# A decoder kernel whose five engines follow written-out orders: the orders, and the hand-out of PSUM banks, written anew

## The chip, the cores and the metric

The kernel runs on one core of a Trainium2 chip. The metric is the time of one launch in device microseconds (us). The kernel before took 5946.84 us, the median of three runs (5941.74 to 5958.27).

## What is computed

The reference is a four-layer decoder over 64 sequences of 128 tokens with 128 channels, all in float32. Each of twelve stages is added to its input and normalised over the channels:

```python
x = _layernorm(x + stage(x, ...), axis=-1)      # twelve times, one stage after the other
```

The stages are, in order and by the names that the kernel uses:

- `rec`: a recurrence over the tokens, solved beforehand for all sequences in an opening phase; of it only a few products are left for the main phase.
- `x0`, `x1`, `x2`: attention with 16 heads of 8 channels from the 128 tokens to a context of 77 rows. `a2`, `a3`, and the first half of `f3`: the same from the tokens to themselves (128 keys).
- `a1`: latent attention with 8 heads, causal. `x3`: attention without a softmax.
- `f0`: a mixture of 8 experts, each taking its 32 best tokens. `f1`: a feed-forward stage with inputs rounded to 4-bit levels. `f2`: a low-rank stage with 6 experts.
- `f3`, second half (`ex`): 8 experts on all tokens, 128 to 512 to 128 channels each.

## The kernel before

**Groups and batches.** After an opening phase (the first 470 us, not touched by the change) the 64 sequences are worked as 16 batches of 4. Three groups of buffers exist, called 0, 1 and 2. Batch i belongs to group i mod 3, so group 0 works six batches one after the other, and groups 1 and 2 five each. Within a group one batch is a single long chain: every stage needs the normalised output of the one before. Work of different groups is independent, and what hides the waits inside one group's chain is the work of the other two.

**Steps.** For each engine a generator (`whole_tensor`, `whole_scalar`, `whole_vector`, `whole_gpsimd`, `whole_sync`) issues one group's instructions in steps, each ended by a `yield`. A batch has 329 steps on TensorE, 255 on ScalarE, 556 on VectorE and 27 on GpSimd. A step begins with its waits on semaphores and then issues one or several instructions.

**The order.** An engine executes its instructions in the order in which they are issued, so one string per engine fixes how the groups' steps stand between one another. `in_order` reads it letter by letter and takes the next step of the group that the letter names:

```python
    for who in order:
        next(programs[who], None)
```

The strings are in the dictionary `ORDER` (line 250). TensorE's has 5264 letters (329 x 16), VectorE's 8896, ScalarE's 4080, GpSimd's 432. SyncE's has 624; there the letters `a` and `b` stand for the two streams of expert weights (256 KB a piece, four places each, `stream_sync`, line 2927), for `f0` and for `ex`. Nothing at run time chooses: if the first instruction of a step must wait, everything behind it on its engine waits as well, of whichever group.

**Banks.** The eight PSUM banks are given out in four pairs. `rec`, `f0`, `a1`, `f1`, `x3` and `ex` take one pair for a group, the other seven stages two. The string `GIVEN` (line 454) lists in pairs of digits which group takes which pair next; `take_banks` (line 1298) makes TensorE wait for the last read by the previous owner.

**Attention.** `attention_tensor` (line 1511) goes through the four sequences of a batch. For each: `scores` (line 1527, 8 matmuls by rows of 32), four maxima on VectorE (`top`, line 1620), the transposition of the maxima (`tops turned`, line 1540), their subtraction from the queries on VectorE (`q shifted`, line 1623), the scores again in the other orientation (`shifted`, line 1555), four exponentials on ScalarE (`p`, line 1607), the product with the values (`out`, line 1577), a copy on ScalarE (`oT`, line 1601), transpositions (`by tokens`, line 1588), and a reciprocal and a product on VectorE (lines 1637 and 1640).

**Experts.** In `gated_tensor` (line 2633) a `hidden` step is one product with 512 columns (line 2646), taken up by ScalarE (line 2674) or VectorE (line 2686) in turn; after each of them stands a quarter of an `expert` step, four products with 128 columns (line 2661). `f0` has similar steps at lines 1902 and 1912. These two kinds of stage are called expert stages below.

Of the kernel before, what the change touches and what calls it, by code (L numbers as in the profile page):

```python
# [212 lines left out]
def memory_layouts(w):  # L213
# [38 lines left out]
        "0000000000000000000000000000000000000000000000000000000000101011111000100101001010101100110010111001"  # L252
        "1001011001110010110000000101001000010100011101122010001101121121121100110111221212220010011001100102"
        "1111210211200112121012002001102212112221121212011200120120110201101000101101000101110010200120110100"
        "1210110020200022012000112011220110002202210100022022221222020002210102000010011200110122122211220000"
        "0100100201221221111212211112211012201011201000122011000220202000101010202102101200122010101101212121"
        "1122112021012020202100202220202022002011110100100110100010110201120120220222200111011011011012021020"
        "1010000210022121021020001000111001000010011010001001100201000202100010211200020210001201002120200200"
        "1002012202112112121222211112122121212111221211211212122001201020102220200202102102021011010101110110"
        "0011011101110010110110110210110210121221112112112201112102121102112111012110110110100110012102122012"  # L260
        "1012000022200200020000202112010020010210201210020222100211002202020221001021002122120010101201202110"
        "2010001110101010120101210220022020202020002021012021222211211121011021122112110020020020211211110111"
        "2121002221211201211002012122002202121010221102202221120102211022022020211212202221201220002221120122"
        "2001022122122221122112212221200102202100121101011011001010111010120021022220200002210202110121201102"
        "1122222221221222120002020121101120120010001100212011121212110220010020100221200112212222222201221021"
        "2022110201001011202202202220022020020201022121022010122012102211122102102012011212120220210100120012"
        "1022002200202202200200220220202002010110101001121122122012210212101000002000000100110020021001101120"
        "0202211220020000202000002002020002000020022200200002002220020022100212210020021221211221112121221121"
        "1222121001210222102111220020120120101020220220200202202002200221010001102101010100111012102120222122"
        "1121210010101100100121001010212000010100012000122012101212211211211011210200202010121121210211121121"  # L270
        "2102011021210210111211010101110210112121200212210211100112211100110211220201121102200200202022202020"
        "0202211201001110102210112002202020202102221221222122121221022201012121022102202001220221121212210212"
        "1221221202202221212220210202200220220122220111011110011011011111102120211200122102110202020202021001"
        "1200112201210120021122121122221121202112002211010011021120120001011201200101122022220012022021012222"
        "2222112121222101000110101011100101012012202202022221210112010211010100022020002200220201022000001220"
        "1000202021020110110122102012100010121122111212122111212212210101200202201012121012120010101001101010"
        "0011101000100101201120210221122122101020101011201210101010021010212010020102120020000202000002001221"
        "1021001021102022100210100200020020200020020010200201002201022000021221212121221211122122112112122100"
        "1201210200110222210100101020222020200222002002202210201001110111001010012122121222102021121101001100"
        "1001001210010120120000100100201202012101021212211211112102211201101211200210212101101211211200101110"  # L280
        "0112112120012101111010112112100112022110220112111112020111012220200202221120112002220200221120210201"
        "0110202000222020020202202202202212222222221222222202122202222022022022022002222221221222222221022221"
        "1011110101121221201220010210210201202020200022202000202220200020222010201002201000120122010111101011"
        "0120112111121011000111201212020200222011100110120122102222112222010020121022002002110100110022022122"
        "1221112221012001200001001010122200221011000220200022002200020200120210102002121201100101121122111122"
        "1221010120020200202020222020202012110100011011100000200202201012212202010110010101012000010100201002"
        "0010010010020100200021110200010022001001001010001001002100100210200010200202110010102121221221121212"
        "2212111201202210112102122100120100120120202022000202220200002202200020220210211201100111212221211212"
        "1210202202220102101010110010100112002100221000212000210020202101212121112122121112122121021010100201"
        "1020221210022012020122200022010212110101012201220221100210110121112211221212111212201021001200120220"  # L290
        "0220020210212020010110121012000110211011201101111111111111111010100110101001101111111101111111101012"
        "1121101100201211201202202222020202200220222012202102102220122110210212210021022020221222120120202102"
        "1022012122021211212212212212112101101011000012210200210220202102020101101112011012012110111111212112"
        "1121020022020202022002202121002112112101001112211121120200202001001020222022211202202222102222210012"
        "0201101001110122202221001012020012202100100221010220120121211221020212001010110221211202122002022002"
        "0220002022202220200020020202210202121121111100000100022002212001220022000010011001002110010020021001"
        "0000120122012021200100011010010001001100100100100120100021121000201211212112212211212122211121220012"
        "0101001220211102101022102002020002202020002202200020200200220221211121001212101110101100100202202200"
        "0000212121001010102010001102102121122012100101000011101001001210212012012201012210102101120020001212"
# [3084 lines left out]
```

## Time and profile before

| | |
|---|---|
| median of three runs | 5946.84 us |
| the profiled execution's own time | 5938.98 us |
| its span, first to last instruction | 5937.1 us |
| TensorE busy with matmuls | 5049.5 us, 85% |
| VectorE busy | 3616.8 us, 61% |
| ScalarE busy | 2391.6 us, 40% |
| mean granted clock of TensorE | 0.913 |

The span is one execution. An engine is busy while it works on an instruction; TensorE's matmuls overlap one another and the loading of weights, so its busy time is not its time at full speed. The granted clock is the share of 2.4 GHz that TensorE was given: it is either 1.0 or 0.5 at a moment, and a mean over a stretch lies between.

### The profile page before, as it was taken

To read this page: it belongs to the slowest core of one execution; us is meant where nothing else is said; L and a number is where in the kernel's file an instruction comes from. 1 tells how busy PE (TensorE), PEld (TensorE's weight loads), DVE (VectorE), ACT (ScalarE), POOL (GpSimd) and SP (SyncE) were. 2 spreads that over 40 slices of the span, in tenths; PEclk is the share of its full clock that TensorE was granted. 3 is DMA by queue.
4 is the path that set the end of the run, shared out by engine and by line. 5 is a ranking of instruction groups with operands and counts; after the bars stand their busy time and mean duration, and the time that the engine had idled before them with its cause. 6 is when DMAs were issued, how large, how long until landed. Compare 5 with 4: busy or idle time off the path is not lost.

```text
span 5937.1 us, 132505 instructions
## 1 busy us (share of the span) xinstructions
PE 5049.5 (85%) x56241; PEld 3711.9 (63%) x56241; DVE 3616.8 (61%) x9657; ACT 2391.6 (40%) x4612; POOL 715.0 (12%) x735
## 2 busy tenths in 40 slices
PE   4756788899898898998789898889889988988897
PEld 3544666567676666766666666756666765665664
DVE  7562567655666666566665665666666566656553
ACT  2112344443434444344344533443543444443431
POOL 6351001101001001000001100000100100000000
PEclk7666799999998999999899999999999988998997
DMA  1112000012010000111001111101001210100010
GB/s 56 25 46 91 30 12 19 7 33 66 13 45 11 30 28 12 56 38 43 26 2 38 32 36 38 58 2 31 19 19 35 64 34 3 36 23 1 14 47 25
DMA packets 144939, 184.71 MB, mean 31 GB/s; under 512 B 46074, under 2 KB 73826, under 8 KB 143714
## 3 DMA queue, kind: packets, MB, share of 16 engines
q1 hardware_dynamic: 144354, 176.23, 9.9%
q8 instruction: 450, 7.37, 0.5%
q14 instruction: 135, 1.11, 0.1%
HBM read 164.32 MB, written 11.57 MB: 30 GB/s over the span
## 4 chain that ended last, share of the span: by engine, by line
PE 67%; DVE 14%; ACT 6%; issue 3%; DMA 1%; POOL 1%; SPq 0%; DVEq 0%; POOLq 0%; ACTq 0%
PE g_bank L2646 8%; PE g_bank L2661 7%; PE g_bank L1555 6%; PE g_bank L1577 6%; PE g_bank L1527 5%; DVE g_tops L1620 4%; ACT g_keys_exps L1607 3%; PE g_bank L1588 3%; PE g_bank L1497 2%; PE g_bank L1902 2%; PE g_bank L2385 2%; PE g_bank L1436 2%; PE g_bank L1993 2%; PE g_bank L1912 1%; PE g_bank L2247 1%
## 5 line engine op out<-in xcount | busy, mean ns | idle before, releaser
L1620 DVE TENSOR_REDUCE g_tops<-g_bank 128x4 f32<-128x308 f32 (+1 forms) x1536 | 812.5, 575 | 413.6 <-PE g_bank L1527 410.9
L1607 ACT ACTIVATE g_keys_exps<-g_bank 77x512 f32<-77x512 f32 (+1 forms) x1536 | 800.3, 596 | 610.8 <-PE g_bank L1555 610.3
L1370 POOL TENSOR_TENSOR g_rstd<-g_rstd,minus_half 128x4 f32<-128x4 f32 x224 | 230.8, 1031 | 4288.9 <-DVE g_rstd L1352 4288.5
L2661 PEld LDWEIGHTS g_bank<-region,g_keys_exps 128*128 128x128 f32 x4096 | 520.4, 192 | 187.8 <-issue 178.9
L2646 PE MATMUL g_bank<-g_xT,region 128*128 128x512 f32 x1024 | 554.7, 624 | 21.8 <-DVE g_keys_exps L2686 12.0
L2661 PE MATMUL g_bank<-region,g_keys_exps 128*128 128x128 f32 x4096 | 545.4, 278 | 11.0 <-DVE g_base L2693 10.7
L1555 PE MATMUL g_bank<-g_qa,g_keys_exps 32*77 32x128 f32 (+1 forms) x12288 | 479.7, 296 | 84.3 <-DVE g_o L1640 55.6
L1555 PEld LDWEIGHTS g_bank<-g_qa,g_keys_exps 32*77 32x77 f32 (+1 forms) x12288 | 400.7, 178 | 197.7 <-DVE g_o L1640 79.0
L1577 PE MATMUL g_bank<-g_keys_exps,g_v 77*32 77x128 f32 (+1 forms) x12288 | 448.8, 291 | 60.5 <-DVE g_tops L1620 58.1
L1527 PE MATMUL g_bank<-g_keys_exps,g_qa 32*128 32x154 f32 (+1 forms) x6144 | 404.7, 377 | 105.1 <-ACT g_keys_exps L1607 91.8
L1601 ACT ACTIVATE g_oT_sc<-g_bank 128x512 f32<-128x512 f32 x384 | 229.5, 598 | 627.2 <-PE g_bank L1577 626.4
L1577 PEld LDWEIGHTS g_bank<-g_keys_exps,g_v 77*32 77x32 f32 (+1 forms) x12288 | 337.0, 116 | 181.2 <-DVE g_tops L1620 125.7
L1527 PEld LDWEIGHTS g_bank<-g_keys_exps,g_qa 32*128 32x128 f32 x6144 | 272.6, 197 | 210.7 <-ACT g_keys_exps L1607 123.4
L2674 ACT ACTIVATE g_keys_exps<-g_bank,region 128x512 f32<-128x512 f32 x256 | 176.0, 688 | 442.4 <-PE g_bank L2646 442.4
L2686 DVE TENSOR_SCALAR g_keys_exps<-g_bank,region 128x512 f32<-128x512 f32 x256 | 191.3, 747 | 265.7 <-PE g_bank L2646 265.3
L1623 DVE TENSOR_TENSOR g_qa<-g_qa,g_bank 128x256 f32<-128x256 f32 x384 | 160.1, 417 | 222.7 <-PE g_bank L1540 220.4
L1588 PE MATMUL g_bank<-consts_sb,g_oT_sc 128*128 128x128 f32 x1536 | 257.4, 293 | 29.1 <-ACT g_keys_exps L1607 18.3
L1588 PEld LDWEIGHTS g_bank<-consts_sb,g_oT_sc 128*128 128x128 f32 x1536 | 179.0, 147 | 108.4 <-issue 60.2
L1379 ACT ACTIVATE g_x<-g_x,g_shift,g_rstd 128x128 f32<-128x128 f32 x384 | 170.4, 487 | 157.8 <-DVE g_shift L1356 157.1
L2646 PEld LDWEIGHTS g_bank<-g_xT,region 128*128 128x128 f32 x1024 | 160.7, 193 | 96.1 <-issue 82.3
L1540 PE MATMUL g_bank<-consts_sb,g_tops 128*128 128x128 f32 x768 | 164.8, 299 | 64.5 <-DVE g_tops L1620 61.0
L1637 DVE RECIPROCAL g_total<-g_bank 128x16 f32<-128x16 f32 x384 | 96.0, 251 | 199.2 <-PE g_bank L1588 198.4
(374 smaller groups left out, 9046.2 us busy)
## 6 DMA issues: line engine op xcount, KB each, us to landing
region<-L_w_in SPq DMA_DIRECT2D x512, 256.0 KB, 2.9
region<-xT_in SPq DMA_DIRECT2D x16, 256.0 KB, 2.8
z_scratch<-m_uT SPq DMA_DIRECT2D x1, 4096.0 KB, 11.0
g_oT_sc<-z_scratch SPq DMA_DIRECT2D x16, 256.0 KB, 3.0
g_xT<-xT_in SPq DMA_DIRECT2D x16, 256.0 KB, 4.1
g_o<-x_in SPq DMA_DIRECT2D x16, 256.0 KB, 4.3
out<-g_x SPq DMA_DIRECT2D x16, 256.0 KB, 2.3
region<-weights_in SPq DMA_DIRECT2D x1, 3020.5 KB, 9.9
```

The costliest lines, as they stand in the source:

```text
L1370: e.tensor_tensor(g.rstd[:, :], g.rstd[:, :], g.s["minus_half"], ALU.pow).then_inc(*b.gpsimd(st + " rstd"))
L1527: ins = e.matmul(bank[r][:, 2 * nk * t:2 * nk * (t + 1)].rearrange("p (i k) -> p i k", i=2), g.qa[rows, t, n, :], g.km[rows, n, t, :, 0:nk ...
L1555: ins = e.matmul(bank[r][0:nk, u * T:(u + 1) * T], g.km[rows, n, t, i, 0:nk], g.qa[rows, t, n, :], start=not masked, stop=not masked or u ...
L1577: ins = e.matmul(b.bank[st][0][32 * u:32 * u + 32, r * T:(r + 1) * T], g.v[0:nk, n, 4 * r + u, :], g.p[0:nk, r, u, :], start=True, stop=True)
L1588: ins = e.transpose(b.bank[st][1][:, r * P:(r + 1) * P], outputs_of(g, n)[:, r, :], g.k["ident"])
L1601: e.activation(outputs_of(g, n - 1), seqs(bank[0][:, :]), ACT.Copy).then_inc(*b.scalar(f"{st} oT {n - 1}"))
L1607: e.activation(g.p[0:nk, r, :, :], bank[r][0:nk, :].rearrange("p (u q) -> p u q", u=4), ACT.Exp, scale=scale).then_inc(*b.scalar(f"{st} p ...
L1620: e.tensor_reduce(g.tops[:, :, first:first + 2], src, AX, ALU.max).then_inc(*b.vector(f"{st} top {n} {r}"))
L2646: e.matmul(bank[0][:, :], weights.part(f"w1 {x}", c), g.xT, start=True, stop=True).then_inc(*b.tensor(f"f3 hidden {k}"))
L2661: ins = e.matmul(bank[1][:, n * D:(n + 1) * D], g.gated_hid[:, x % 2, c, n * T:(n + 1) * T], weights.part(f"w2 {x}", c), start=c == n == 0 ...
L2674: e.activation(g.gated_hid[:, k // HC % 2, k % HC, :], b.bank["ex"][0][:, :], ACT.Relu, bias=g.w["f3_b1"][:, k:k + 1]).then_inc(*b.scalar( ...
L2686: e.tensor_scalar(g.gated_hid[:, x % 2, k % HC, :], b.bank["ex"][0][:, :], g.w["f3_b1"][:, k:k + 1], 0.0, ALU.add, ALU.max).then_inc(*b.ve ...
```

## The change

Only strings change: all five strings of `ORDER` and `GIVEN`. No instruction is added, taken away or altered; each engine has the same steps, each group's steps stand in the same order among themselves, and the lengths of the strings and the counts of each letter are the same. What differs is how the groups' steps are interleaved on each engine, at which places of the weight streams the groups' own loads stand on SyncE, and which pair of banks each stage uses.

Of TensorE's string the first 200 letters and letters 4701 to 5264 (each line has 100):

```diff
     "tensor": (
-        "0000000000000000000000000000000000000000000000000000000000101011111000100101001010101100110010111001"
-        "1001011001110010110000000101001000010100011101122010001101121121121100110111221212220010011001100102"
...
-        "0000212121001010102010001102102121122012100101000011101001001210212012012201012210102101120020001212"
-        "1012000000202020020022022000020222020002012001021121121221110001002102010012211101110101122120210010"
-        "0120122010200200200200022020002022020201010020202001211212101201011210101010112101000110111201100011"
-        "0110201101201101112112101100010110110100111010011100110112112112211011002002002020022220200222220220"
-        "0202222022000220222202200022022020220202200022222022022022022220202200200000000000000000000000000000"
+        "0000000000000000000000000000000000000110010010011001010110010010010000010101110100110010001111001011"
+        "0011100011001001021200211221211120011112112211121021112011200120212000212211211211122221121202110202"
...
+        "2201120001120110110110210101111112121011011112102111221022012101010020201112112020112100121122020002"
+        "0000020202020222022002002020022200202002220202022200202022202002220020200002222000220222002220220200"
+        "0000022220200022022020022220200200200002222202220202220200200202200020202020020020202202200020020200"
+        "0022000220202022200202022202000202202000000202002222020002022022020022202002220022022222222222020020"
+        "0200200202220222020222202202020222202202002202202200202000000000000000000000000000000000000000000000"
         "0000000000000000000000000000000000000000000000000000000000000000"),
```

So on TensorE group 1 begins at letter 38 (before: 59) and group 2 at letter 118 (before: 148); group 1 ends at letter 4792 (before: 5070) and group 2 at letter 5155 (before: 5171). On VectorE group 1 begins at letter 77 (before: 79) and group 2 at 191 (236); group 1 ends at letter 8115 (8651) and group 2 at 8753 (8779), of 8896.

The beginnings of SyncE's string and of `GIVEN`:

```diff
     "sync": (
-        "000000111111222222aabbabbaaaaaaaaaaaaaaaaaaaaaaaaaaaaaaaaaaaaaaaaaaaaaaaaabbbbbbbbbbbbbbbb0000000bbb"
+        "000000111111222222bbabaabaaaaaaaaaaaaaaaaaaaaaaaaaaaaaaaaaaaaaaaaaaaaaaaaabbbbbbbbbbbbbbbb0000000bbb"
...
 GIVEN = (
-    "00010203101201130013022121220013000213112200011301001322110001131221002002031011230011122322111110222300"
+    "00010203101211001321222100130122110013220003110300111220230201131022010022231011032203200110112223022311"
```

## Rows read from the trace of the kernel before

**Rows 1.** The page: span, busy times, and the span in 40 slices (tenths busy; PEclk granted)

```profile
span 5937.1 us, 132505 instructions
PE 5049.5 (85%) x56241; PEld 3711.9 (63%) x56241; DVE 3616.8 (61%) x9657; ACT 2391.6 (40%) x4612; POOL 715.0 (12%) x735
...
PE   4756788899898898998789898889889988988897
...
PEclk7666799999998999999899999999999988998997
```

**Rows 2.** The page: the chain that ended last, by engine

```profile
PE 67%; DVE 14%; ACT 6%; issue 3%; DMA 1%; POOL 1%; SPq 0%; DVEq 0%; POOLq 0%; ACTq 0%
```

**Rows 3.** Waits: who waited for whom, us in total, times, longest us

```profile
PE g_bank L1527 <- ACT g_keys_exps L1607: 91.8, 75, 3.7
PE g_bank L1540 <- DVE g_tops L1620: 61.0, 61, 3.3
PE g_bank L1577 <- DVE g_tops L1620: 58.1, 88, 2.0
PE g_bank L1555 <- DVE g_o L1640: 55.6, 53, 2.6
...
PE g_bank L1680 <- DMA g_xT<-xT_in: 28.8, 7, 18.3
```

**Rows 4.** Timeline, one attention round of group 0 alone: start, us, engine, line, count [idle before]

```profile
499.08 0.42 DVE L1623 TENSOR_TENSOR g_qa<-g_qa,g_bank 128x256 f32<-128x256 f32 x1 [1.49 <-PE g_bank L1540]
...
499.56 2.00 PE L1555 MATMUL g_bank<-g_qa,g_keys_exps 32*77 32x128 f32 x32 [0.51 <-DVE g_qa L1623]
501.63 2.04 ACT L1607 ACTIVATE g_keys_exps<-g_bank 77x512 f32<-77x512 f32 x4 [2.54 <-PE g_bank L1555]
...
503.72 1.41 PE L1527 MATMUL g_bank<-g_keys_exps,g_qa 32*128 32x154 f32 x16 [2.16 <-ACT g_keys_exps L1607]
505.20 1.64 DVE L1620 TENSOR_REDUCE g_tops<-g_bank 128x4 f32<-128x308 f32 x4 [5.70 <-PE g_bank L1527]
...
505.74 1.94 PE L1577 MATMUL g_bank<-g_keys_exps,g_v 77*32 77x128 f32 x32 [0.60 <-DVE g_tops L1620]
```

**Rows 5.** Windows, eleven stretches with an expert stage under way: length, busy by engine, PEclk

```profile
core 0: us, PE busy (x) PEld busy (x) DVE busy (x) ACT busy (x) POOL busy (x), PEclk, DMA share, GB/s
1147.00:1261.90 114.90, 111.26 (x1060) 79.04 (x1061) 65.28 (x151) 41.77 (x74) 9.46 (x7) 1.00 0.12 36
...
sum 1292.30, PE 1259.41 PEld 901.73 DVE 781.18 ACT 465.40 POOL 79.42; mean PE 114.49 PEld 81.98 DVE 71.02 ACT 42.31 POOL 7.22
```

**Rows 6.** Windows, thirteen stretches with three groups and no expert stage

```profile
904.50:1147.00 242.50, 202.10 (x2506) 143.61 (x2505) 171.94 (x454) 116.86 (x215) 24.00 (x21) 0.98 0.01 4
...
2839.10:3102.70 263.60, 212.04 (x2682) 153.11 (x2681) 179.51 (x465) 117.88 (x221) 22.65 (x20) 0.91 0.01 3
...
5307.50:5576.60 269.10, 217.51 (x2666) 155.78 (x2664) 174.46 (x430) 115.93 (x214) 27.61 (x24) 0.89 0.01 1
sum 2353.80, PE 1961.65 PEld 1415.77 DVE 1569.92 ACT 1080.99 POOL 231.19; mean PE 150.90 PEld 108.91 DVE 120.76 ACT 83.15 POOL 17.78
```

**Rows 7.** Windows, the main phase by the number of groups at work

```profile
470.70:571.70 101.00, 66.71 (x559) 51.24 (x560) 25.73 (x81) 26.32 (x48) 11.49 (x14) 0.66 0.24 75
571.70:690.00 118.30, 91.93 (x968) 68.31 (x967) 63.49 (x162) 39.26 (x74) 8.52 (x8) 0.74 0.02 6
...
876.00:5181.00 4305.00, 3828.59 (x42752) 2813.49 (x42751) 2705.48 (x7276) 1865.69 (x3419) 386.62 (x349) 0.95 0.10 30
5181.00:5685.00 504.00, 431.95 (x4792) 318.65 (x4791) 294.97 (x817) 218.36 (x401) 44.36 (x39) 0.92 0.05 15
5685.00:5780.00 95.00, 91.01 (x739) 63.17 (x738) 52.62 (x139) 32.24 (x54) 11.78 (x10) 1.00 0.16 48
5780.00:5848.70 68.70, 42.42 (x401) 30.84 (x399) 25.88 (x80) 16.88 (x32) 5.21 (x5) 0.59 0.03 8
...
sum 5466.40, PE 4778.33 PEld 3506.79 DVE 3320.51 ACT 2298.67 POOL 480.29; mean PE 597.29 PEld 438.35 DVE 415.06 ACT 287.33 POOL 60.04
```

**Rows 8.** Groups by line on TensorE: count, busy us, mean ns, idle before

```profile
L2646 PE MATMUL g_bank<-g_xT,region 128*128 128x512 f32 x1024 | 554.7, 624 | 21.8 <-DVE g_keys_exps L2686 12.0 <-ACT g_keys_exps L2674 7.4
L2661 PE MATMUL g_bank<-region,g_keys_exps 128*128 128x128 f32 x4096 | 545.4, 278 | 11.0 <-DVE g_base L2693 10.7
```

More of the change, by code:

```diff
@@ L257 @@
[L257 to L266, printed above, removed]
@@ new lines @@
+        "2001100120220000220020220101001110110221001020022000001000202120102201010101122102000201010001010102"
+        "0120102121122121221112122121121222000200222020200211210210011100101212212121221201121000001000210111"
+        "1212101101022202202020202000202202000202202020020221211121221001010120120121211120202020020200202022"
+        "0020220220002022202020102012012110201101101012222112121212212221111220120110110010012121201202212200"
+        "2200012000112100100120002000201202102110122002102010020020022002000221020120100200100011010000100011"
@@ new lines @@
+        "1200010221211111121210010000022012001202210121011010010111010010110111101101001101110121101201121011"
+        "2110121211211120110221211210111211202111011012100200112211200200200000000002011200101211221200010211"
+        "2001202012212201220101222010222122011102012202012221120012012202022121200210122102202222012202012001"
+        "2022020222210212020112011221210110101011011110100110221120210220102222211212111021012020020110010211"
+        "0221121101202111220110002001121201210102120120101011010001011010001011100100201201011001210110002002"
@@ new lines @@
+        "0221010001101121201100022022221220000202122210200020220020012010101001102122221221210210012010020100"
+        "1212101122121122110120120120112020011220102002010100100101210210202122101121221112121221100120212201"
+        "2002212211121221010211000010101110012202020202202200011101111101012000002012010121221012201201001011"
+        "0100010011100100102010010202010012000211020120001210202021020002000212012002011100221012201002001200"
+        "1002000210021100010212121112212211121222112100121202200201212012011020120110110111101010101111011100"
@@ new lines @@
+        "0110111101100011101110201211202112021021111202110212201112120110210100101001110000110112002202220220"
+        "2002000200211211110100200121201020200202200220020220202210010210201212211001021211021020101110120020"
+        "1220120121210200022000020220200020220202011222122221201200210010011001121121111011112102202112112102"
+        "1002002201201211012012212022021202202112212202202020121022021220210201220212120202211000210221122220"
+        "0021102212221221010222120101101011000101011000011011010220120101122212101000120220200002002020210121"
@@ new lines @@
+        "2111212212210002000000102222120102022201011110101010010011010010010101201201020011112120021201021121"
+        "2212220212012102222001222212001221010011001011011000101110101001201221022102022000212111210012210100"
+        "1220102011000020211000212002000020020000101221010012101201012010201002210120200100100101000001001011"
+        "0001000010000111212121212121211002021220100210120200220202120120111100101010100011000101002012210121"
+        "2020212210101101211100110002002001001002002200202012012100010212012112112011210120011020101011211200"
```

345 lines of the change are left out of this document (165 added, 180 removed).

## The prediction

> **What bounds the kernel now.** I read the page first, then the chain, the waits, windows, and one attention round in the timeline. TensorE is busy for 85% of the span, VectorE for 61%, ScalarE for 40% [rows 1], and the chain that ended last is 67% TensorE, 14% VectorE and 6% ScalarE [rows 2]. So TensorE sets the time, but not alone: in the main phase it has gaps, and the gaps are many and short. The four largest causes of waiting on TensorE make 267 us in 277 waits, none over 3.7 us [rows 3]. All four stand in attention, and the round of group 0 alone shows where they come from [rows 4]: after "shifted" (2.00 us) TensorE stands still for 2.16 us until the exponentials are done, after "scores" (1.41 us) for 0.60 us until the first maximum is. With other groups' steps between them these waits vanish. The change decides nothing but that: which steps stand between.
>
> Two kinds of stretch follow from this. With an expert stage under way TensorE is busy for 1259.41 of 1292.30 us, 97%, at a granted clock of 1.00 in nearly all [rows 5]: an expert batch offers long steps that wait little (32.8 us of waits before 1100 us of matmuls) [rows 8]. With three groups at work and none in an expert stage it is busy for 1961.65 of 2353.80 us, 83%, at about 0.92 [rows 6]. Two groups in the ramp: 78% at 0.74. One group alone in attention at the end: 62% at 0.59 [rows 7].
>
> **How I weigh an order.** For each of a batch's 329 TensorE steps I took from the trace how far it moved the end of TensorE's work, waits not counted, as the median over the 16 batches. The sum is 281 us a batch and 4499 us in all; I call it work. It can be laid along either string. In the trace of before a unit of it cost this much time: with three groups and an expert stage 1.03, with three and none 1.30, with two and none 1.71 (the ramp only, at a low clock), with two and an expert stage 1.05, with one and none 2.7, with one in experts 1.27. A second tally, the cover: for each step, the least time that in this trace passed since its group's previous TensorE step ended (its need), less the other groups' work that stands between them in the string. Laid along the old string the missing cover sums to 690 us; TensorE was idle for 688 us of the main phase (5466.40 less 4778.33) [rows 7], 670 of them between its steps. In pieces of 50 steps the two run together (correlation 0.93). With only two groups the tally says 36 us where 26 were idle, a factor of 0.72, since one stall there also covers the other group's need.
>
> **The change, part by part.** No instruction is added or removed, so every busy time at a given clock stays; what can move is idle time and clock.
>
> *The ramp (steps 1 to 147).* Group 1 joins at step 38, not 59, and group 2 at 118, not 148. Before, this part took 220 us for 114 us of work [rows 7]. After: 27 us of work alone, 40 with two groups, 22 with two and `f0`'s experts, 24 with three. By the prices above 27 x 2.8 + 40 x 1.71 + 22 x 1.05 + 24 x 1.15 = 195, so 25 us less; by the cover 13 us less (54 for 67). The clock of the ramp is low whichever the order, so I take 15 us less, bounds 0 and 25.
>
> *The middle (steps 148 to 4600, always three groups).* Steps beside an expert stage: 1902 before, 1967 after, because two expert stages fall on each other less often (144 steps before, 69 after, over the whole string). In work 68 us move from price 1.30 to 1.03: 18 us less. Missing cover: 520 us before, 497 after, 23 us less. Part of the needs is only bounded, since before the step never waited; on those that did wait (400 us before) it is 36 us less, on the others (119) 13 more. Busier stretches also have the higher clock [rows 5, 6]. I take 25 us less. Bounds: 80 less, if the foreign VectorE, ScalarE and GpSimd work inside the groups' chains counts too (715 us of it between a TensorE step and its successor before, 642 after, a tenth less; TensorE idled 500 us there, and a tenth of it with its clock is 50 to 60), and 20 more, if the fine mixture loses what the coarse one gains.
>
> *The end (steps 4601 to 5264).* This speaks against the change. Group 1 now ends 278 steps earlier, and from step 4792 to 5154 groups 0 and 2 are by themselves. 243 of these steps (208 us of work) stand beside no expert stage, in attention, `f0` to `f2` and `a3`. Before there were none such: the two groups' stretch was beside group 2's experts, 91.01 us busy of 95.00 [rows 7]. The last 94 steps, group 0 in `f3`, are the same in both; before them group 0 now has 16 more steps alone (14 us of work). Before, this part took 748 us. After, by the prices: 128 x 1.03 + 36 x 1.30 + 108 x 1.05 + 40 x 2.7 + 60 x 1.27 = 476, and 208 times the price of two groups without experts. That price is the open one. As three groups have it, 1.30: 270, and the end takes 746. As in the ramp, 1.71: 356, and it takes 832. The cover misses 100 us in this stretch, times 0.72 is 72, a price of 1.35, and the clock makes it a little more; I take 1.43, which gives 773, 25 us more. Bounds 0 and 85.
>
> The trace shows what such gaps do besides: with group 0 alone in attention the granted clock is 0.59, mostly the lower of its two levels (1.2 of 2.4 GHz), and it was 1.00 in the 95 us before, when TensorE was 96% busy [rows 7]. The Trainium skill ("TensorE: Matmul & The Clock Gate", section "HAM oscillation — how this bites in real kernels") says that waits inside a loop can send the array back to the low clock again and again. By that rule the two groups' stretch would come out nearer to the ramp's price than to that of three groups; this is the slow rival below, whose price comes from rows 7 and not from the page.
>
> *SyncE and banks.* SyncE's loads and stores stand at other places, and a wait for a weight place holds back what is behind it. Between the TensorE step that frees a load and the step that needs it I count under 5 us of work for 107 of 560 loads before and 102 after; TensorE's largest DMA wait, 28.8 us, is mostly the first load, which stays [rows 3]. I take 0, bounds 10 either way. The bank pairs go by the same order of stages, and a hand-over that comes late is in the cover already: 0.
>
> Sum: -15 - 25 + 25 + 0 = -15 us. The profiled execution took 5939 us, so it would take 5924; the median of the runs is 8 us above it. The two tallies differ by some 20 us, and the one that costs the string by its coarse kinds gives about 0 for the middle and end together, so I round the gain down: 5935 for the median.
>
> **The rivals.**
>
> *Faster, 5890.* The tenth less of foreign work inside the chains is worth its 50 to 60 us of idle time and clock in the middle, and the end costs as three groups do: 5947 - 15 - 45 + 0, rounded. For it: three of the four large waits on TensorE are for VectorE [rows 3], and VectorE's order changed as much as TensorE's. Against it: in this trace the foreign work inside a chain adds nothing to what cover alone explains of the idle time (fitted together its weight is about zero).
>
> *Slower, 5990.* The two groups without experts run at the ramp's price of 1.71, and the middle gives 10 us only. 5947 - 15 - 10 + 85 is 6007; with a price of 1.63 it is 5990. From a price of 1.50 on the whole is no longer a gain; beyond 1.60 it is slower than can be missed. For it: 243 steps of serial stages with a clock that falls. Against it: the ramp's clock had the thin first 100 us behind it.
>
> *It does not do what it says.* The waits are set by the chains within a group and by the four bank pairs, and another interleaving gives as many: 5947, within the forecast's range.
>
> **How the numbers follow.** Two runs of this kernel tell apart what differs by more than 0.3%, 18 us. The forecast, no change that can be measured, has 0.37, with the case that nothing happens in it; its own range is 5929 to 5965. Faster has 0.36, slower 0.27. The range that leaves out one in ten on either side is 5872 to 6005: on the low side the bounds -25, -80 and 0 would give 5842, all at once and unlikely; on the high side 0, +20 and +85 would give 6052, likewise.
>
> **What would show it.** Right, if after the change TensorE's busy time stays within 1% of 5050 us, the ramp until group 2's first step is 20 to 40 us shorter, the middle is 83% busy without experts and 97% with, and from group 1's end the stretch of two groups outside experts is 70 to 75% busy at a clock near 0.85. Wrong on the fast side, if the waits for VectorE in rows 3 shrink by more than a fifth; wrong on the slow side, if that last stretch is under 68% busy or has a clock under 0.75.

## The result

The changed kernel takes 5867.32 us, the median of four runs (5859.01 to 5880.25), against 5945.26 us (5941.74 to 5958.27) for the kernel before on the same chips: a ratio of 0.9867, 95% interval 0.9843 to 0.9891. It is faster by 78 us, and the forecast of 5935 was wrong: it lay 68 us above, and the range ended at 5872. The profiled execution took 5880.25 us, the slowest of the four, so the two traces show 59 us of the 78.

### The profile after

The page: span, busy times, slices, and the chain that ended last. They answer to [rows 1] and [rows 2].

```profile
span 5878.4 us, 132510 instructions
PE 5043.8 (86%) x56241; PEld 3693.5 (63%) x56241; DVE 3629.9 (62%) x9657; ACT 2401.9 (41%) x4617; POOL 711.6 (12%) x735
...
PE   4766888899988899899898988989888898997787
...
PEclk7576889999989999999999999999989999998987
...
PE 69%; DVE 12%; ACT 7%; issue 2%; DMA 1%; POOL 1%; SPq 0%; POOLq 0%; DVEq 0%; ACTq 0%
```

TensorE works nearly as long as before (5043.8 for 5049.5 us) in a shorter span; most of what went is idle time. VectorE's share of the chain fell from 14% to 12%. ScalarE has five instructions more, 4617 for 4612, although the change adds none. They come back below.

The main phase can be cut at the same places of TensorE's string in both traces: steps 1 to 147 (the ramp), 148 to 4600 (the middle), 4601 to 5264 (the end). As the strings differ, the same places do not hold quite the same steps: the ramp has 1367 matmuls for 1530, the middle 44746 for 44716, the end 6433 for 6302. The windows of before, then of after; columns as in [rows 5]:

```profile
470.70:690.70 220.00, 159.34 (x1530) 120.25 (x1531) 89.22 (x243) 66.28 (x124) 20.02 (x22) 0.70 0.12 38
690.70:5177.20 4486.50, 3980.54 (x44716) 2926.80 (x44715) 2827.22 (x7600) 1951.58 (x3580) 396.90 (x359) 0.95 0.10 30
5177.20:5924.50 747.30, 638.45 (x6302) 459.74 (x6300) 397.55 (x1088) 279.07 (x504) 61.35 (x54) 0.90 0.07 22
```

```profile
471.50:661.20 189.70, 145.08 (x1367) 112.30 (x1366) 83.10 (x226) 66.83 (x121) 20.04 (x23) 0.74 0.17 55
661.20:5085.90 4424.70, 3968.86 (x44746) 2911.64 (x44742) 2833.10 (x7594) 1958.61 (x3586) 396.70 (x359) 0.95 0.10 30
5085.90:5865.70 779.80, 653.23 (x6433) 460.61 (x6432) 410.67 (x1110) 281.77 (x507) 57.50 (x53) 0.89 0.08 23
```

The number behind the two times is the stretch's length. Ramp: 30 us shorter (forecast 15). Middle: 62 us shorter (forecast 25); TensorE's busy time there is 12 us less, its idle time 50 us less. End: 32 us longer (forecast 25). Together 60 us less.

The waits of TensorE, which answer to [rows 3]:

```profile
PE g_bank L1527 <- ACT g_keys_exps L1607: 77.6, 72, 3.7
PE g_bank L1577 <- DVE g_tops L1620: 54.8, 90, 1.5
...
PE g_bank L1540 <- DVE g_tops L1620: 46.0, 51, 3.7
PE g_bank L1555 <- DVE g_o L1640: 40.6, 41, 2.4
PE g_bank L1680 <- DMA g_xT<-xT_in: 40.2, 11, 18.1
...
PE g_bank L2000 <- DVE g_keys_exps L2061: 18.7, 17, 3.2
```

The three waits for VectorE in [rows 3] made 174.7 us and now make 141.4, a fifth less. One that the forecast had not looked at, line 2000 (attention a1), fell from 46.6 to 18.7. Over all lines of the main phase TensorE's waits for VectorE fell from 408 to 346 us. The largest single one, for ScalarE's exponentials, fell from 91.8 to 77.6, but over all lines the waits for ScalarE did not fall (237 us for 231), and the wait for the input loads (line 1680) rose from 28.8 to 40.2. So the idle time that went is that of the waits for VectorE.

With the steps laid over the traces by their matmuls, and an expert stage counted from its first `hidden` step to its last `expert` step, the middle splits into 2775 us without an expert stage and 1713 us beside one before, 2668 and 1757 after. TensorE's idle time fell from 456 to 410 us in the first kind and from 50 to 46 in the second.

### The profile page after: what moved, and what is told of

Read it like the earlier page. It is cut to its first block, busy times and chain, and to the rows that moved or that the text cites. A ratio compares the mean times of both kernels' runs of the same rounds, so it can differ in the third digit from the quotient of the medians.

```text
span 5878.4 us, 132510 instructions
## 1 busy us (share of the span) xinstructions
PE 5043.8 (86%) x56241; PEld 3693.5 (63%) x56241; DVE 3629.9 (62%) x9657; ACT 2401.9 (41%) x4617; POOL 711.6 (12%) x735
## 4 chain that ended last, share of the span: by engine, by line
PE 69%; DVE 12%; ACT 7%; issue 2%; DMA 1%; POOL 1%; SPq 0%; POOLq 0%; DVEq 0%; ACTq 0%
PE g_bank L2646 8%; PE g_bank L2661 8%; PE g_bank L1555 7%; PE g_bank L1577 6%; PE g_bank L1527 6%; ACT g_keys_exps L1607 4%; DVE g_tops L1620 3%; PE g_bank L1497 3%; PE g_bank L1588 2%; PE g_bank L1436 2%; PE g_bank L1902 2%; PE g_bank L1912 2%; PE g_bank L2385 1%; PE g_bank L1993 1%; PE g_bank L1391 1%
## 5 line engine op out<-in xcount | busy, mean ns | idle before, releaser
L1607 ACT ACTIVATE g_keys_exps<-g_bank 128x512 f32<-128x512 f32 (+1 forms) x1536 | 799.9, 596 | 629.0 <-PE g_bank L1555 628.1
L1527 PE MATMUL g_bank<-g_keys_exps,g_qa 32*128 32x154 f32 (+1 forms) x6144 | 402.3, 375 | 94.0 <-ACT g_keys_exps L1607 77.6
L2693 DVE SCALAR_TENSOR_TENSOR g_base<-g_bank,g_gates,g_base 128x128 f32<-128x128 f32 x512 | 148.9, 341 | 66.7 <-PE g_bank L2661 60.6
```

The source lines that it names most:

```text
L1527: ins = e.matmul(bank[r][:, 2 * nk * t:2 * nk * (t + 1)].rearrange("p (i k) -> p i k", i=2), g.qa[rows, t, n, :], g.km[rows, n, t, :, 0:nk ...
L1607: e.activation(g.p[0:nk, r, :, :], bank[r][0:nk, :].rearrange("p (u q) -> p u q", u=4), ACT.Exp, scale=scale).then_inc(*b.scalar(f"{st} p ...
```

## The experiments

Every kernel here has the steps of before; strings alone differ, and each diff shows the first line that differs in one of them. The times of "before" beside which a run is measured differ by a few microseconds from one set of runs to the next (medians 5946.0, 5942.32 and 5939.21), so distances are best taken by the ratios. "Rearranged" means: with a replay of the strings (every step takes its median duration from the trace of before, waits are those of the semaphores, the bank pairs and the order, and the clock is left out) letters were moved about by trial as long as the replayed time fell. The replay gives 5276 us for the main phase of before, where the trace shows 5454, and only its differences are used. Whatever is given as the replay's is a computed figure and no run.

### Same TensorE order, other engines by a rule

`t_before_rule` keeps TensorE's string and the banks of before. The other engines take at each point the step that can start first, the lowest group at a tie.

```diff
     "vector": (
-        "0000000000000000000000000000000000000000000000000000000000000000000000000000001000010000001011111101"
+        "0000000000000000000000000000000000000000000000000000000000000000000000000000001000000000010100011111"
```

> TensorE's string and the banks as before; the strings of VectorE, ScalarE, GpSimd and SyncE are written anew by one plain rule: whichever group's next step can start earliest goes next (durations of steps from the trace of before). Theory C (the cover on TensorE explains the idle time, foreign work on the other engines weighs nothing, as the prediction took it): TensorE's string is the same, so the missing cover is the same 690 us, and the time stays within 0.5% of before, 5920 to 5970. Theory V (what stands inside a group's chain on the other engines counts as much as what stands on TensorE): the plain rule lets long steps of other groups in ahead of short urgent ones, and the time rises by 2 to 4%, 6060 to 6190.

Measured: 6243.65 us, ratio 1.0491 (1.0455 to 1.0526). `t_after_rule` is the same rule beside the changed kernel's TensorE string:

```diff
     "vector": (
-        "0000000000000000000000000000000000000000000000000000000000000000000000000000111111111111111111111110"
+        "0000000000000000000000000000000000000000000000000000000000000000000000000001011111111111111111111110"
```

> TensorE's string and the banks as in the changed kernel; the other four strings by the same plain rule as in t_before_rule. If the gain of the change sits in TensorE's interleaving, this is 60 to 90 us (1.0 to 1.5%) below t_before_rule. If it sits in the order of the other engines, which the rule takes away in both, the two are within 0.3% of each other. By theory C it is also within 0.5% of the changed kernel's 5867; by theory V it is 2 to 4% above it.

Measured: 6131.58 us, ratio 1.03 (1.0265 to 1.0335). With TensorE's string held fixed the time moved by 298 us. With the rule held fixed the new TensorE string, with its banks and with the strings that the rule writes beside it, is 112 us faster than the old one. In the windows of `t_before_rule` nearly all of the loss lies in the middle, at the same steps as above:

```profile
472.50:692.60 220.10, 157.35 (x1529) 118.70 (x1530) 88.87 (x243) 65.94 (x124) 20.40 (x22) 0.72 0.12 38
692.60:5488.90 4796.30, 4083.99 (x44717) 3001.50 (x44716) 2822.97 (x7600) 1998.89 (x3615) 395.03 (x359) 0.92 0.09 28
5488.90:6242.40 753.50, 637.75 (x6302) 456.11 (x6300) 396.73 (x1088) 279.07 (x504) 61.69 (x54) 0.91 0.07 21
```

The middle is 310 us longer: idle time 712 for 506 us, and busy time 4084 for 3981 us at a clock of 0.92 for 0.95. A third of the loss is this longer busy time at a lower clock. (ScalarE also has 34 more table loads than before, 44 us at 1283 ns each; see below.) The missing cover, which reads TensorE's string only, is 690 us for this kernel as for before. Its waits for VectorE in the main phase are 522 us for 408:

```profile
PE g_bank L1527 <- ACT g_keys_exps L1607: 111.8, 80, 3.7
PE g_bank L1555 <- DVE g_o L1640: 71.1, 54, 3.5
PE g_bank L1540 <- DVE g_tops L1620: 70.4, 56, 4.4
PE g_bank L1577 <- DVE g_tops L1620: 61.7, 87, 4.1
```

They are not more frequent (56 for 61, 87 for 88), but longer (at most 4.4 for 3.3, 4.1 for 2.0 us). VectorE is not alone in this: over all lines the waits for ScalarE rose nearly as much, from 231 to 335 us. The rule rewrote four strings at once, so this run shows that the other engines' order counts, not which engine's.

### The tie rule

`due_before` and `due_after` differ from these two by the choice among steps that can start: the one whose result TensorE's string needs first goes first. The string of banks is new in both as well, which the expectations do not say: in 10 of its 320 hand-outs (`due_before`) and in 4 (`due_after`) a pair comes from another previous owner than in the kernel whose TensorE string it has.

```diff
     "vector": (
-        "0000000000000000000000000000000000000000000000000000000000000000000000000000001000010000001011111101"
+        "0000000000000000000000000000000000000000000000000000000000000000000000000000001000010000000110001111"
```

> TensorE's string as before; the other strings by a rule that differs from t_before_rule in one thing: among the steps that could start at the same moment because their engine is what they wait for, the one that TensorE's string needs first goes first, where the plain rule took the lowest group number. Theory D (this choice is what the other engines' strings are worth): nearly all of the plain rule's 298 us are gone, 5910 to 5960. Theory W (the amount of foreign work inside the chains decides): that amount is the same as in t_before_rule (579 us, 582 there, 817 before), so the time is the same, 6200 to 6250, or by the tally even under before.

> TensorE's string as in the changed kernel, the others by the rule of due_before. By theory D this is the changed kernel's time within 0.5% (5840 to 5890), and its distance to due_before, 0.8 to 1.3%, is what TensorE's string alone is worth with equally good strings beside it. If the change's gain were in its VectorE string, due_after and due_before would be within 0.3%.

Measured: `due_before` 5990.49 us, ratio 1.0083 (1.0068 to 1.0097); `due_after` 5938.9 us, 0.9995 (0.9983 to 1.0007). Against `t_before_rule` and `t_after_rule` the new tie rule, with those few banks, took off 253 and 193 us. Table loads do not explain this, since `due_before` has 110 of them for 102. Between the two, with one rule, the kernel with the new TensorE string is again faster, by 51 us; it also has 14 loads fewer (96 for 110). Both still stand behind the kernels whose TensorE string they have, by 45 and 72 us. They have 42 and 23 more table loads than these, 54 and 30 us of ScalarE's time; `act_only` below bears on that. For `due_after` at least the larger part of the 72 us stays open.

### VectorE alone

`v_only` is before with VectorE's string rearranged and nothing else.

```diff
     "vector": (
-        "0000000000000000000000000000000000000000000000000000000000000000000000000000001000010000001011111101"
+        "0000000000000000000000000000000000000000000000000000000000000000000000000000000100100000000111111110"
```

> The kernel before with VectorE's string alone replaced: letters moved by a few places, one at a time, wherever a replay of the strings with the step durations of the trace of before came out shorter. All other strings and the banks are those of before, so work beside experts, ramp, end and missing cover are untouched. Theory C: no change, within 0.3% of 5945. Theory V: VectorE's order alone is worth as much as the whole change or more: 70 to 110 us less, 5835 to 5875.

Measured: 5877.32 us (5863.01 to 5883.62), ratio 0.9874 (0.9843 to 0.9904). One engine's string, and not TensorE's, is worth what the whole change is. Its windows at the same steps, then its waits:

```profile
472.60:692.70 220.10, 161.88 (x1530) 121.68 (x1531) 90.96 (x243) 66.36 (x124) 20.00 (x22) 0.69 0.12 38
692.70:5132.20 4439.50, 3974.11 (x44717) 2913.39 (x44716) 2820.68 (x7600) 1954.04 (x3580) 394.42 (x359) 0.95 0.10 31
5132.20:5869.20 737.00, 634.87 (x6302) 454.21 (x6300) 395.68 (x1088) 279.14 (x504) 61.23 (x54) 0.91 0.07 22
```

```profile
PE g_bank L1527 <- ACT g_keys_exps L1607: 90.1, 76, 3.9
...
PE g_bank L1577 <- DVE g_tops L1620: 54.7, 88, 2.7
PE g_bank L1540 <- DVE g_tops L1620: 54.5, 62, 3.0
PE g_bank L1555 <- DVE g_o L1640: 47.9, 55, 2.2
PE g_bank L2000 <- DVE g_keys_exps L2061: 40.6, 24, 7.3
```

The ramp is as long as before, the middle 47 us shorter, the end 10. The wait for ScalarE stays (90.1 for 91.8), those for VectorE shrink while their number hardly changes (441 for 453 over all lines); together they make 358 us for 408. The tally that the prediction took for VectorE's part, foreign work inside the chains, would have said slower: 892 us here for 817 before.

### ScalarE alone, and the table loads

ScalarE computes its activation functions from a table, and must load another one when the next function is not in the one it has. `act_only` is before with ScalarE's string alone rearranged; the replay did not yet know these loads and gave 20 us less.

```diff
     "scalar": (
-        "0000000000000000000000000000000000000000000000001110001100110100111111111001111100111111001000001100"
+        "0000000000000000000000000000000000000000000000001110001100101100111111111001111100111111001000001100"
```

> The kernel before with ScalarE's string alone replaced, by one that the first replay, in which ScalarE's steps have fixed durations, called 20 us shorter. But it changes between stages that need different activation functions more often: by the order of the steps 105 changes of function table for 67 in the main phase, and a load of a table took 1283 ns in every trace. Theory L (these loads stand in the way of steps that TensorE waits for): 38 more loads are 49 us of ScalarE, and with the 20 us gained the time rises by 20 to 50 us, 5965 to 5995. If ScalarE, 60% idle, hides them: 20 us less, 5915 to 5930.

Measured: 5988.61 us, ratio 1.0098 (1.0065 to 1.0131), 49 us slower. ScalarE's groups of table loads in before (the first fence; count, busy us, mean ns of one) and here:

```profile
L1938 ACT ACT_TABLE_LOAD x19 | 24.4, 1283 | 0.3
L1607 ACT ACT_TABLE_LOAD x19 | 24.4, 1283 | 0.3
L2292 ACT ACT_TABLE_LOAD x16 | 20.5, 1283 | 0.3
```

```profile
L1938 ACT ACT_TABLE_LOAD x37 | 47.5, 1283 | 0.7
L1607 ACT ACT_TABLE_LOAD x35 | 44.9, 1283 | 0.6
L2292 ACT ACT_TABLE_LOAD x16 | 20.5, 1283 | 0.3
```

`f0`'s Gelu (line 1938), the exponentials of attention (1607) and `f2`'s logarithm (2292) need three tables. A load stands wherever two steps with different tables follow each other, so its count is a property of ScalarE's string: 68 in before, 73 after (the five more instructions), 104 here. With the loads put into the replay, 1283 ns each, it gives before 5276, `act_only` 5305, and for the changed kernel 5216. So of the 69 us between the first replay and the chip the loads explain 49, by the replay; 20 stay open. In the trace TensorE's waits for ScalarE rose by 33 us (264 for 231). No run changes the number of loads and nothing else. The timeline of ScalarE in before shows one load (start, us):

```profile
2126.38 0.69 ACT L2674 ACTIVATE g_keys_exps<-g_bank,region 128x512 f32<-128x512 f32 x1
2127.08 1.28 ACT L2292 ACT_TABLE_LOAD   x1
2128.37 0.63 ACT L2292 ACTIVATE g_o<-g_o 128x512 f32<-128x512 f32 x1
```

The activation before ends 0.02 us ahead of it, the next begins 0.01 us behind it. All 68 loads of this trace start within 0.02 us of the end of the activation before, and 59 have the next within 0.1 us. The Trainium skill ("ScalarE: Activation LUTs", section "What ACT_TABLE_LOAD costs") gives 1283 ns as well, but adds a drain of 1380 ns to every switch; the trace has the first and no room for the second here.

### All strings rearranged, without and with the loads

Without the loads counted, all strings and the banks (`all_long`, the diff against the changed kernel), and those of VectorE, ScalarE and GpSimd alone (`a_sec`, likewise):

```diff
     "tensor": (
-        "0000000000000000000000000000000000000110010010011001010110010010010000010101110100110010001111001011"
+        "0000010100000000000000000000000000100000001001100011011000010010100010000110110110010001001111001011"
```

> All five strings and the banks rearranged by the same moves, from the changed kernel's as the start. If the replay holds for orders far from those it was taken from, this is 3.5 to 4.5% below before (5680 to 5740) and below the changed kernel too. If its gain is fitted to the third digit of durations that vary from run to run, most of it is lost and the time is 5800 to 5870.

```diff
     "vector": (
...
-        "0101110100000000000011111110000001011101110101001010001111111111111001110101001010111111102011012000"
+        "0101111000000000000011111110000001011101110011001010001111111111111001111100101010101111101010020201"
```

> TensorE's string and the banks as in the changed kernel; the strings of VectorE, ScalarE and GpSimd rearranged letter by letter in the replay, as VectorE's was in v_only. v_only gave 69 us less than before from one string; if the two gains add up, this is 50 to 90 us below the changed kernel, 5780 to 5820. If the changed kernel's strings already hold what v_only found, it is within 0.4% of 5867.

Measured: `all_long` 5791.38 us, 0.9734 (0.9706 to 0.9762); `a_sec` 5909.14 us, 0.9947 (0.9929 to 0.9966), slower than the changed kernel whose TensorE string it has, with 107 loads for 73. The replay does not explain this: with the loads counted it puts `a_sec` 19 us below the changed kernel, and the chip 45 above. And `all_long`, with 103 loads, is faster than either. So many loads can go with a fast order, and what makes `a_sec` slow is open.

With the loads counted, the strings of VectorE, ScalarE and GpSimd alone (`t_before_best`, the diff against before), and all strings and the banks (`best`, against the changed kernel):

```diff
     "scalar": (
-        "0000000000000000000000000000000000000000000000001110001100110100111111111001111100111111001000001100"
+        "0000000000000000000000000000000000000000000000001110001100101100111111111001111100111111001000010100"
```

> TensorE's string and the banks as before, the strings of VectorE, ScalarE and GpSimd rearranged by a replay that counts the table loads (71 for 67 before). By that replay 111 us less; the kernels so far gave three quarters of what a replay promised for rearranged strings, so 70 to 110 us less, 5835 to 5875. If TensorE's string, the same as before, held the kernel, under 0.5% would be left (5915 or more), and the change could not have been matched without it.

```diff
     "tensor": (
-        "0000000000000000000000000000000000000110010010011001010110010010010000010101110100110010001111001011"
+        "0000000000000000011000000000000000000100110001000101010001010010100001000110110110100100001111001011"
```

> All five strings and the banks rearranged, with the table loads counted (80 loads; all_long had 102). By the replay 270 us less than before. With three quarters of it: 200 us less, 5740 (5710 to 5770), below all_long (5791). If the loads are hidden and do not matter, the same as all_long, 5780 to 5800.

Measured: `t_before_best` 5854.27 us, 0.9861 (0.9834 to 0.9887), 72 loads; `best` 5741.45 us (5730.77 to 5742.37), 0.967 (0.9644 to 0.9696), 79 loads. So with the old order of TensorE and SyncE and the old banks the kernel is as fast as the changed one, and between `t_before_rule` and `t_before_best` one TensorE string has run at 4.9% above and 1.4% below the same kernel. `best` beats both: 198 us under before. Its windows at the same steps:

```profile
471.00:666.00 195.00, 148.78 (x1374) 115.44 (x1374) 83.51 (x226) 66.27 (x121) 20.52 (x23) 0.76 0.17 53
666.00:4957.60 4291.60, 3930.54 (x44776) 2870.28 (x44772) 2826.19 (x7596) 1945.65 (x3589) 398.20 (x361) 0.97 0.10 31
4957.60:5727.90 770.30, 650.63 (x6402) 456.19 (x6402) 411.32 (x1109) 281.36 (x508) 56.33 (x52) 0.90 0.08 25
```

Its middle has 361 us of idle time for 506, and at a clock of 0.97 its busy time is another 50 us less. Its waits for VectorE make 229 us. Group 1 ends early in it too (letter 4793 for the change's 4792), and its end is longer than before as well (770 for 747).

### The two halves of the change

`first_new` has the new strings until TensorE's step 1474 and the old ones behind it, `rest_new` the reverse. Line 15 of TensorE's string in `first_new`, against after:

```diff
-        "1212101122121122110120120120112020011220102002010100100101210210202122101121221112121221100120212201"
+        "1212101122121122110120120120112020011220102002010100100101101001101110000012011212120220210100120012"
```

> The first 1474 steps on TensorE (28% of the main phase), and the matching stretch of the other engines, in the changed kernel's order, the rest in that of before; there the two orders are within six steps of each other. If the gain comes evenly along the string with the ramp on top: ramp 29 us and 1326 steps of the middle at 62 us per 4453 make 47 us less, 5890 to 5910. If all of it were the earlier ramp and head: 70 us less, 5870 to 5880. If the gain sits behind: within 0.3% of before.

> The reverse of first_new: before's order for the first 1474 steps on TensorE, the changed kernel's for the rest. The change gave 78 us and first_new 43 of them. If the parts add up this gives the other 35: 5895 to 5925. If the new end (two groups without experts) eats what the middle gains, it is within 0.3% of before, 5930 or more.

Measured: `first_new` 5899.62 us, 0.9937 (0.9913 to 0.9961); `rest_new` 5933.18 us, 0.9994 (0.9975 to 1.0013). By parts, ramp / 148 to 1474 / 1475 to 4600 / end, in us: before 219 / 1339 / 3148 / 747; after 190 / 1332 / 3093 / 780; `first_new` 192 / 1332 / 3129 / 743; `rest_new` 223 / 1371 / 3084 / 781. The ramp's gain goes with the first half and the end's loss with the second, each as it is in the change. The middle does not add up: `rest_new` took 1371 us for steps 148 to 1474, where it has the strings of before but for the last few steps, which took 1339, at a clock of 0.93 for 0.96. Part of this is the choice of execution: the profiled one of `rest_new` is 13 us above its median, that of `first_new` 17 us below. By medians the halves give 43 and 6 us (5899.62 and 5933.18 against 5942.32 and 5939.21), and together they give 78. The 29 us between are not explained; by the intervals the halves can give up to 52 and 15 us and the change as little as 65, so they may be chance.

### The replay against the chip

Change against before in us, replay with loads / measured median: after -60 / -78; `v_only` -78 / -69; `t_before_best` -111 / -85; `best` -270 / -198; `all_long` -187 / -155; `first_new` -26 / -43; `rest_new` -22 / -6; `a_sec` -79 / -33; `due_after` -18 / -3; `act_only` +29 / +49; `due_before` +59 / +48; `t_after_rule` +119 / +186; `t_before_rule` +220 / +298. The sign is right for all thirteen, of which `rest_new` and `due_after` are too near to zero to count. Between two rearranged kernels it can be wrong, as with `a_sec` and the changed kernel. The misses are 46 us or less but for `best` and the two rule kernels. The tally of cover gives the same number for all five kernels that have before's TensorE string and other strings beside it, whose times lie between 1.4% below and 4.9% above before.

## Why the prediction was wrong

**The step that failed is the middle.** The prediction took 25 us, from the missing cover (23) and the price of steps beside experts (18), and weighed only TensorE's string. The middle gave 62: 50 us of idle time and 12 of busy time. It had the bound (80 less) and the rival for it, and set the weight of the other engines' strings to about zero, since in one trace the foreign work in the chains explained nothing beyond cover. The runs show both halves of that to be wrong. The other strings do count: VectorE's alone gave 69 us, and beside one TensorE string they move the time by some 380 us (4.9% above before to 1.4% below). And foreign work is the wrong measure: by the tally it is 892 us in `v_only`, which is faster than before, and 579 in `due_before`, which is slower (817 in before). Which of the steps that could start goes first counts for far more: with one tie rule for another, at the same foreign work, 253 us. In one trace the other strings do not vary apart from TensorE's, which is the likely reason why the fit gave them no weight; no run tests that.

**Which string the gain in the middle comes from** is open. At one rule the new TensorE string, with what the rule writes beside it, gave 51 us (`due_*`) and 112 us (`*_rule`), over all parts of the phase, against 78 for the whole change. TensorE's waits for VectorE fell by 62 us, but either engine's order can do that. So TensorE's string may well carry most of the change's gain; then the cover, which reads that string, is what was too small. The plain test would be the old strings of the others beside the new one of TensorE. No run has them: in the replay the two come to a standstill, since each waits for steps that the other's order has behind.

**The ramp** was mis-sized, not wrong: 30 us for 15. The tally by prices had 25 (it uses 2.8 for one group alone where the list of prices has 2.7, and 1.15 for three, which the list does not have; with 2.7 it is 28). I cut it to 15 on the ground that the clock is low there whichever the order. It was 0.74 for 0.70, and from group 1's first step to group 2's, with `f0`'s experts now among the steps, it was 0.84, where two groups had 0.74 before [rows 7]:

```profile
471.50:550.30 78.80, 48.86 (x418) 34.18 (x418) 24.00 (x80) 17.99 (x35) 10.50 (x14) 0.56 0.14 46
550.30:636.40 86.10, 71.81 (x763) 57.06 (x761) 45.47 (x118) 34.35 (x62) 7.43 (x7) 0.84 0.16 50
```

TensorE's busy time in the ramp fell by 14 us, but this is not the clock alone, since the part now holds 163 matmuls fewer. Group 2's first step came 166 us after the start for 219: 53 us earlier, where the prediction's sign of being right named 20 to 40.

**The end** was right: 32 us for 25. Steps of both groups outside expert stages fill the window 5310 to 5560; behind it stand the 125 us beside group 2's experts, and group 0 alone:

```profile
5310.00:5560.00 250.00, 194.46 (x2374) 134.96 (x2374) 145.65 (x364) 101.08 (x185) 16.57 (x15) 0.87 0.01 1
5560.00:5685.00 125.00, 116.41 (x944) 82.63 (x942) 64.47 (x171) 42.10 (x73) 11.76 (x10) 0.96 0.11 33
5685.00:5866.00 181.00, 134.41 (x850) 87.52 (x850) 54.64 (x159) 37.17 (x65) 8.32 (x8) 0.75 0.07 21
```

The first is 78% busy at 0.87, where 70 to 75% near 0.85 was forecast. As an estimate of the price, its length over busy time times clock is 250 / (194.46 x 0.87) = 1.48; the same for the ramp's two groups is 118.3 / (91.93 x 0.74) = 1.74 [rows 7], near the 1.71 of the prediction. So the price was close to the forecast 1.43 and far from the slower rival's. `first_new`, with the old end, has 743 us there, so the loss belongs to these strings.

**SyncE and banks** were forecast at 0, and `t_before_best` and `v_only` keep both of before and are as fast as the change, so a gain of this size does not need them; what they gave within the change is not measured. The wait for the input loads rose by 11 us, the one sign of SyncE's string, about the bound of 10.

**The rivals.** The slower one named the right place and too high a price: the end cost near to what was forecast, and the other two parts gave more than it took. The faster one, 5890, came nearest. Its reason (other engines' order makes TensorE wait less) held, its measure did not, and it still took too little for ramp and middle. Its sign was in the list, waits for VectorE in [rows 3] down by more than a fifth, and was just missed: they are down by 19%; at line 2000, which the list had left out, by 60%. The signs for the forecast itself did not tell the cases apart: TensorE's busy time stayed within 1%, and the middle was 85% busy without experts and 97% with, close to the 83% and 97% named. "It does not do what it says" is out: another interleaving gives fewer waits.

**The table loads** were in no term. In this change there are only five more, 6.4 us of ScalarE. `act_only`, whose order ignores them, lost 49 us where 20 were to be won.

## What to carry to other kernels

Where queues are fixed by hand, an estimate from the bounding engine's order alone is blind to much: 4.9% above and 1.4% below came from one TensorE order here. Replay all queues together with the durations of the trace, and take its figures as a direction: the chip gave at least 73% of what it promised where that was over 60 us, but for `a_sec`, and a difference of 19 us between two good orders had the wrong sign. Where ties on the helper engines have to be broken by a rule, what the bounding engine needs next beat the lowest number. Count what the order itself creates: an activation table load of 1283 ns stands wherever neighbours on ScalarE need different tables. And if a cause does not vary by itself in the trace at hand, a fitted weight of zero for it is no evidence; keep its bound as a case with its full chance.

## What was not expected of the hardware

- Interleaving decides the number of table loads: 68, 73, 79, 104 and 107 in kernels with the same activations, 1283 ns each, with no drain beside them in the timeline.
- Idle time and a lower clock go together. Where TensorE's idle time in the middle was 712, 506, 456 and 361 us (`t_before_rule`, before, after, `best`), its mean granted clock was 0.92, 0.95, 0.95 and 0.97, and nearly the same matmuls took 4084, 3981, 3969 and 3931 us. With the clock at three digits (0.923, 0.950, 0.955, 0.971) busy time times clock is 3771, 3783, 3791 and 3817 us, so the shorter busy time is the higher clock.
- Nearly the same strings over steps 148 to 1474 took 1339 us in one execution and 1371 in another, at 0.96 and 0.93 (before and `rest_new`).
